# Sampling a 64 x 64 x 512 tensor along its sequence: matmuls with one-hot matrices, or gathers from DRAM

## What is computed

```python
x = x + L0(x, cond)   # modulated RMS norm, 16-head attention (q, k normed), projection
x = x + L1(x, cond)   # linear sampling, below
x = x + L2(cond, x)   # GRU over 64 steps
x = x + L3(cond, cond, x)   # Runge-Kutta steps of a coupled oscillator over 64 steps

# L1: input is x as (N, C, L) = (sequence, token, channel), grid is cond
ix = (grid + 1.0) * 0.5 * (L - 1)
x0 = jnp.floor(ix); w1 = ix - x0; w0 = 1.0 - w1
i0c, i1c = jnp.clip(x0, 0, L - 1), jnp.clip(x0 + 1, 0, L - 1)
v0 = jnp.take_along_axis(input, i0c[:, None, :], axis=2)
v1 = jnp.take_along_axis(input, i1c[:, None, :], axis=2)
return w0[:, None, :] * v0 + w1[:, None, :] * v1
```

## Time and profile before

| | us |
|---|---|
| median of 3 runs | 1828.99 |
| lowest, highest | 1824.32, 1829.84 |
| the profiled execution | 1831.36 |
| its span in the profile | 1829.4 |

### The profile page before, as it was taken

One profiled execution on the slowest core, in us unless ns is written; L12 is line 12 of the kernel. 1 busy time (PEld: TensorE's weight loads), 2 busy tenths in 40 slices (PEclk: granted clock), 3 DMA queues, 4 the chain that ended last, 5 costly groups with the idle time before them and its releaser, 6 DMA issues.

```text
span 1829.4 us, 100329 instructions
## 1 busy us (share of the span) xinstructions
PE 1593.6 (87%) x44506; PEld 1398.0 (76%) x44506; DVE 1582.0 (86%) x3935; ACT 821.4 (45%) x1886; POOL 697.0 (38%) x832
## 2 busy tenths in 40 slices
PE   5778778788878787885799999999999999999995
PEld 4355555556555555555799999999999999999995
DVE  5699999999999999986289888888988988899887
ACT  3533333323333333333255555555555555555553
POOL 2333333333333333334433444434443344434342
PEclk9889999999999999997799999999999999999999
DMA  5200010000000000002000000000000000000000
GB/s 183 93 16 23 25 25 18 24 23 25 26 25 17 25 23 26 20 13 80 6 10 14 13 14 16 14 13 14 13 15 15 13 13 15 15 14 13 14 15 15
DMA packets 91905, 45.47 MB, mean 25 GB/s; under 512 B 75984, under 2 KB 84240, under 8 KB 91472
## 3 DMA queue, kind: packets, MB, share of 16 engines
q1 hardware_dynamic: 91024, 39.03, 8.9%
q0 software_dynamic: 448, 0.02, 0.1%
HBM read 30.56 MB, written 8.45 MB: 21 GB/s over the span
## 4 chain that ended last, share of the span: by engine, by line
PE 49%; DVE 1%; issue 1%; POOL 0%; ACT 0%; POOLq 0%; ACTq 0%; DVEq 0%
PE ps_RZ L1032 20%; PE ps_F L1059 13%; PE ps_N L1032 10%; PE ps_F L1064 6%; DVE ps_S L1199 0%; DVE rest L1199 0%; DVE ts L1224 0%; DVE cub L1228 0%; ACT ps_T L1096 0%; POOL en L1337 0%; DVE ps_E L1199 0%; DVE qst L1199 0%; DVE Qs L1323 0%; DVE Hf L1220 0%; DVE P L1316 0%
## 5 line engine op out<-in xcount | busy, mean ns | idle before, releaser
L1059 PE MATMUL ps_F<-ts,Cp 128*128 128x64 f16 x8192 | 283.2, 193 | 12.7 <-ACT ts L1096 11.5
L825 PE MATMUL psQ<-Wx,front 128*128 128x512 f16 x1152 | 285.6, 401 | 1.2 <-issue 1.2
L1059 PEld LDWEIGHTS ps_F<-ts,Cp 128*128 128x128 f16 x8192 | 257.5, 98 | 14.6 <-ACT ts L1096 12.4
L634 DVE TENSOR_SCALAR E<-rows,lidx 128x512 f16<-128x512 f16 x512 | 229.4, 500 | 0.0
L1096 ACT ACTIVATE ts<-qst 128x256 f16<-128x256 f32 x192 | 80.1, 417 | 311.1 <-DVE qst L1199 311.1
L825 PEld LDWEIGHTS psQ<-Wx,front 128*128 128x128 f16 x1152 | 115.7, 103 | 133.7 <-issue 29.6
L1032 PE MATMUL ps_RZ<-xs,Wx 128*128 128x64 f16 x6144 | 204.0, 194 | 3.8 <-POOL xs L1341 2.4
L1032 PE MATMUL ps_RZ<-hs,Whh 128*128 128x64 f16 x6144 | 201.6, 193 | 1.3 <-POOL hs L1337 0.4
L1032 PEld LDWEIGHTS ps_RZ<-xs,Wx 128*128 128x128 f16 x6144 | 191.0, 99 | 5.5 <-POOL xs L1341 2.9
L1032 PEld LDWEIGHTS ps_RZ<-hs,Whh 128*128 128x128 f16 x6144 | 188.5, 98 | 2.4 <-issue 1.6
L1064 PE MATMUL ps_F<-ts,Cp 128*128 128x64 f16 x4096 | 163.0, 193 | 1.0 <-issue 0.3
(11 more groups left out here) (167 smaller groups left out, 3515.3 us busy)
## 6 DMA issues: line engine op xcount, KB each, us to landing
front<-in_x SPq DMA_DIRECT2D x32, 256.0 KB, 3.6
rows<-rows_dram SPq DMA_DIRECT2D x64, 128.0 KB, 3.0
out<-ot SPq DMA_DIRECT2D x512, 16.0 KB, 1.8
XR<-in_L_cond_W_qkv SPq DMA_DIRECT2D x4, 768.0 KB, 16.3
E<-in_L_cond_W_hh SPq DMA_DIRECT2D x4, 768.0 KB, 4.4
front<-in_L_cond_W_ih SPq DMA_DIRECT2D x4, 768.0 KB, 5.8
XR<-in_L_cond_W_emb SPq DMA_DIRECT2D x1, 2048.0 KB, 11.0
E<-in_L_cond_coupling SPq DMA_DIRECT2D x1, 1024.0 KB, 5.5
```

The source lines that it names most:

```text
L634: e = v.tensor_scalar(E[b][:, t, c, :], rows[b][:, :], lidx[:, t, c:c + 1], None, ALU.is_equal)
L825: last = mm(psQ[:, n, :], xn[p.u][:, i, c, :], Wqkv[:, j, c, n * D:(n + 1) * D], start=(c == 0 and t == 0), stop=(c == KC - 1 and t == 2))
L1059: mm(psF[:, s % 2, m, :], Cp[:, i, c, m * PART:(m + 1) * PART], ts_[:, 0, c, :], start=(c == 0 and m == 0 and i == 0), stop=False, skip_gr ...
```

## The change

The sampling is done by gathers instead of matmuls.

- After `residual`, x1 of a pair goes to DRAM (`store_x1` on SP, four DMAs of 128 KB): a buffer of 513 rows of 128 floats per sequence, in which row r holds channel r-1 in its left half and channel r in its right half, so that one row holds both taps for all 64 tokens.
- GpSimd issues 8 indirect DMAs per pair (`gather`), each fetching 128 rows of 512 bytes. They stand first in its slot, for pair i-3. The indices (`idx`) are transposed in `setup` as integers; i0 is capped at 510 with the weight going to the second tap.
- VectorE mixes the taps for pair i-4 in 16 instructions, `first_tap` and `second_tap`, within the Newton steps. The second writes XR.
- `residual` writes a contiguous tile x1; `keep_xT` writes one of five contiguous tiles. `build_tap`, `sample`, `weigh_taps`, `add_taps`, `high_x1`, `low_x1`, `load_rows` and E are gone. There is one slot more.
- x is loaded for pair i+3 instead of i+2.
- `setup` fills the four DRAM buffers with zeroes and waits for that.
- In the recurrences, the seeds and the bias are held narrow and are read with a stride of zero along the batch.

```diff
+        def store_x1(p):
+            sp.wait_ge(x1_done, p.n + 1)
+            for tap in range(2):
+                for b in range(2):
+                    rows = x1_dram[p.u * 2 + b][1 - tap:1 - tap + D, tap * T:(tap + 1) * T]
+                    sp.dma_start(rows.rearrange("(c p) t -> p c t", p=PART), x1[p.u][:, :, b, :]).then_inc(x1_out[p.u], 16)
...
         def slot(pair, i):
-            if p := pair(2):
+            if p := pair(3):
                 load_x(p)
...
-            if p := pair(-2):
-                load_rows(p)
...
             if i == NP:
                 for c in range(KC):
                     load_wih(c)
+            if p := pair(-2):
+                store_x1(p)
...
+        def gather(p):
+            pool.wait_ge(x1_out[p.u], p.half * 64 + 64)
+            pool.wait_ge(whh_lo, KC)
+            need(pool, x2_done, p.n - 1)
+            for b in range(2):
+                for c in range(KC):
+                    pool.indirect_dma_start(G[p.u][:, b, c, :], None, x1_dram[p.u * 2 + b],
+                                            bass.IndirectOffsetOnAxis(ap=idx[:, c, p.n * 2 + b:p.n * 2 + b + 1], axis=0))\
+                        .then_inc(gathered[p.u], 16)
...
         def slot(pair, i):
+            if p := pair(-3):
+                gather(p)
             if p := pair(1):
                 low_x(p)
...
-            if p := pair(-3):
-                add_taps(p, 0)
             if p := pair(-1):
                 norm_p(p)
-            if p := pair(-3):
-                add_taps(p, 1)
-            if p := pair(-2):
-                low_x1(p)
             if p := pair(2):
                 shift_x(p)
...
+        def first_tap(p, k):
+            b, c = k // KC, k % KC
             if k == 0:
+                dve.wait_ge(gathered[p.u], p.half * 128 + 128)
+                need(dve, x2_done, p.n)
+            v.scalar_tensor_tensor(out=um[:, b, c, :], in0=G[p.u][:, b, c, 0:T], scalar=WT[:, 0, c, p.n * 2 + b:p.n * 2 + b + 1],
+                                   in1=x1[p.u][:, c, b, :], op0=ALU.mult, op1=ALU.add).then_inc(tap0_done, 1)
+
+        def second_tap(p, k):
+            b, c = k // KC, k % KC
+            dve.wait_ge(tap0_done, p.n * 2 * KC + k + 1)
+            last = v.scalar_tensor_tensor(out=XR[:, :, c, p.n * 2 + b], in0=G[p.u][:, b, c, T:2 * T],
+                                          scalar=WT[:, 1, c, p.n * 2 + b:p.n * 2 + b + 1], in1=um[:, b, c, :],
+                                          op0=ALU.mult, op1=ALU.add)
             if k == 2 * KC - 1:
+                last.then_inc(x2_done, 1)
...
             for k in range(STEPS):
-                if tap and k + EARLY < 2 * KC:
-                    build_tap(tap, 1, k + EARLY)
+                if tap and k < 2 * KC:
+                    first_tap(tap, k)
+                if tap and k >= LAG:
+                    second_tap(tap, k - LAG)
```

More of the change, by code:

```diff
@@ L11 @@
 I32 = mybir.dt.int32
+U32 = mybir.dt.uint32
 WS = 64.0
@@ L60, in program @@
 def program(nc, x, cond, W_emb, b_emb, g_norm, W_qkv, g_q, g_k, W_out, W_ih, W_hh, b_ih, b_hh,
-            coupling, bias, out, rows_dram):
+            coupling, bias, out, x1_dram):
     B, T, D = x.shape
@@ L252, in _ @@
         last.then_inc(w1_T, 1)
+        pe.wait_ge(rows_ready, 1)
+        for c in range(KC):
+            last = nc.tensor.transpose(psI[:, c, :], irow[:, c * PART:(c + 1) * PART], ident[0:B, 0:B])
+        last.then_inc(idx_T, 1)
         pe.wait_ge(cond_kept, 1)
@@ L259, in _, with attention_and_sampling @@
         last.then_inc(emb_done, 1)
-def attention_and_sampling(nc, ctx, XR, ident, keep, later, x, rows_dram, W_out, coupling, W_hh, W_ih):
+def attention_and_sampling(nc, ctx, XR, ident, keep, later, x, x1_dram, W_out, coupling, W_hh, W_ih):
     B, T, D = x.shape
@@ L438, in norm_p @@
                 .then_inc(p_done, 1)
[L440 to L445, removed]
-            last.then_inc(x1_ready, 1)
         def shift_x(p):
@@ L592, in slot @@
                 keep_xT(p)
-            if p := pair(-2):
-                high_x1(p)
             if i == -1:
@@ L733, in slot @@
         def slot(pair, i):
-            x, qk, tap = pair(2), pair(0), pair(-3)
+            x, qk, tap = pair(2), pair(0), pair(-4)
             n = x.n if x else qk.n + 2 if qk else None
             cols = slice(QK.start if qk else X.start, X.stop if x else QK.stop)
-            for k in range(EARLY):
-                if tap:
-                    build_tap(tap, 1, k)
             if qk:
@@ L765, in slot @@
                 subtract_max(p)
-            if tap:
-                weigh_taps(tap, 0)
             if p := pair(-1):
                 sum_p(p)
-            if tap:
-                weigh_taps(tap, 1)
-            if p := pair(-2):
-                for k in range(2 * KC):
-                    build_tap(p, 0, k)
             if x:
@@ L922, in slot @@
                 project(p, 1)
-            if i == NP:
-                sample(pair(-3), 0)
-                sample(pair(-3), 1)
             if p := pair(-1):
@@ L933, in slot @@
                 scores(p)
-            if (p := pair(-3)) and i != NP:
-                sample(p, 0)
-                sample(p, 1)
             if p := pair(-2):
@@ L1445 @@
     out = nc.dram_tensor("out", shape, F32, kind="ExternalOutput").ap()
-    rows = nc.dram_tensor("rows_dram", (shape[0], shape[2]), F16, kind="Internal").ap()
+    rows = [nc.dram_tensor(f"x1_dram{k}", (shape[2] + 1, 2 * shape[1]), F32, kind="Internal").ap() for k in range(4)]
     program(nc, *args, out, rows)
```

145 lines of the change are left out of this document (50 added, 95 removed).

## The result

The changed kernel took **1949.97 us** (median of 4 runs, 1946.59 to 1953.59) against 1827.42 (4 runs, 1824.32 to 1829.84) for the kernel before: ratio 1.067, 95% interval 1.064 to 1.070. It is slower; the forecast was 1762, range 1700 to 1825. The kernel before takes much the same time in every job, 1821.6 to 1832.6; the changed one has two times, 1945.7 to 1950.0 in two jobs and 1720.8 in a third, and its executions in one job agree within 0.4%.

The account below looks back on a forecast made before the run. VectorE was taken to set the attention stage's 25.0 us slot. A period of 22.8 over 29 slots saved 64 us and the tail 3: 1831.4 - 67 = 1764, with the median 2.4 lower, 1762 us; range 1700 to 1825.

Parts of the forecast that it names:

- GpSimd's side: GpSimd's queue per slot: eight gathers at 1.1 us each, then `low_x`; costs nothing up to 1.6 us each.
- rival C: Gathers hold VectorE's Newton steps: 7 to 8 us more per slot, period near 29, about 1940 us; chance 0.08.
- Price of an issue: One indirect DMA issue on GpSimd: 1.1 us, bounds 0.5 and 3; eight take 8.8.
- Store: x1's way to DRAM, from `residual`'s end to the gathers' start: 6 us, bounds 3.0 and 12.
- Steps and taps: VectorE's Newton steps with 16 taps laced in: 6.45 us per slot, 2.3 of it for taps (bounds 1.6 and 4.5).
- Path and clock: Chain of waits through one slot: 21.55 us, plus 1.2 for TensorE's lower clock: period 22.8, bounds 21.0 and 25.
- Removal from VectorE: VectorE's work per slot: 7.35 us removed (sampling 6.7, `residual` 0.64), 2.3 added by the taps.
- Tail: End of the attention stage, after the last pair's `low_v`: 68.3 us becomes 65, so -3, bounds -12 and +15.
- the sum: Whole kernel: 29 slots save 64 us and the tail 3, so 1831.4 - 67 = 1764; median 1762 us.

Follow-up runs that it names:

- c1: The changed kernel itself, unchanged, timed again in another job on chip 12: 1720.8 us, ratio 0.943 to the kernel before.
- e7: The changed kernel with its 16 taps at the start of VectorE's slot, not among the Newton steps: 1946.5 us.
- e3: The changed kernel with the third `project` of a pair put between the two halves of `mix`: 1731.5 us.
- e11: The changed kernel with each of `mix`'s 96 matmuls using the whole array instead of a 64 by 32 tile (other values): 1959.8 us.

## Why the prediction was wrong

The gap to the kernel before is 1945.6 - 1829.4 = 116.2 us of span: 31 periods give (968.1 - 77.1) - 775.3 = 115.7, the rest 0.5. Against c1 it is 226.5: 31 periods give 891.0 - 672.6 = 218.4, or 7.0 a slot. The idle time ahead of L848 grew by more, 284.9 - 7.1 = 277.8 or 9.0 a slot: some 2 us a slot of it stand where TensorE is idle elsewhere in c1. That the "remote" part alone, 216.2, is near 218.4 is chance.

- **The step that failed** is "GpSimd's side". It gave the eight indirect DMAs a price in GpSimd's queue (1.1 each, "costs nothing up to 1.6") and on VectorE (rival C), and none on TensorE. They made the slot 7.0 us longer through TensorE on some chips, and held it not at all on others. The trace of before has no indirect DMA, so the price could not be read; but only two of the engines were bounded, and the others were taken as free.
- **Rival C** gave 1940 us and a period near 29, and 1950 and 28.7 were measured, with its mechanism false: the steps with all their taps took 518.81 to 524.41, 5.6 us, beside the gathers. The right number was luck.
- **Price of an issue**: pitch 1.25 (0.96 and 0.30 between), 10 us for eight instead of 8.8. It stayed free, as said: on c1 GpSimd waits 145.8 us in 31 slots for `rden`, 4.7 each.
- **Store**: from `residual`'s end to the first gather 4.2 us (519.85 to 524.04 in c1), 6 forecast.
- **Steps and taps**: 5.6 us measured, 6.45 forecast. In the kernel before, the 5.14 held 0.5 for the builds and 1.0 for the step under `low_x`, in every middle slot; in c1 and in the changed kernel no step is held in the middle slots, where I gave back only half (0.5). So the bare steps are 5.14 - 0.5 - 1.0 = 3.64, and sixteen taps cost some 2.0, 0.12 each; e7, with its taps elsewhere, has 3.6 from the first step to `scale_qk` in the median slot, against 5.4 with them, which gives 1.8. I took 2.3, within my bounds. The estimate by the formula of the Trainium skill's "VectorE: DVE Perf Modes", section on the TRN2 errata, was 3.6; the rows speak against it where independent instructions follow.
- **Path and clock**: c1's period is 21.70. The path summed to 21.55, and the 1.2 for TensorE's clock was added on top. The clock did fall as forecast (0.88, I said 0.90), so its cost is in the 21.70 and others were too large, the steps with their taps by 0.85 among them. That the rest agrees to some tenths is not shown term by term.
- **Removal from VectorE**: busy 91.39% of 25.0 = 22.8 us a slot before, 74.01% of 21.70 = 16.1 on c1: 6.8 less, where 7.35 - 2.3 = 5.05 was forecast; the hold of 1.0 that is gone is part of the rest.
- **Tail**: from the last `sum_p` to the end 1829.4 - 855.5 = 973.9 before, 967.4 on c1: -6.5, where -3 was forecast; 977.5 in the changed kernel.
- On c1 the whole is 1719.1 - 1829.4 = -110 us where the sum said -67: its 1720.8 us lie within the stated range, below the forecast's 1730 to 1800. The path held as far as the period shows it, and the largest mis-sized term is that period (21.7, not 22.8: 34 us over 31 slots).

## What to carry to other kernels

An instruction form that the trace of before doesn't hold has an unknown price on every engine, not only on the one that issues it; bound each, or run a small kernel with it first. Measure such a change on more than one chip, and put the two kernels that are to be compared into one job: a difference between jobs can be the chip's (e3's time looked like an effect of its order for two jobs). And when an instruction's cost is worked out from a stretch, take out of it first what else was held there: the 1.0 us of `low_x` would halve the price of the taps. Put long issues of GpSimd where its tensor instructions would otherwise meet VectorE's short two-input ones: by that the kernel with gathers was 0.9 us a slot faster than the one without, where TensorE wasn't held.

## What was not expected of the hardware

- Indirect DMAs of GpSimd (128 rows of 512 B, 0.96 us each) hold TensorE on some chips: after some 45 to 60 matmuls from the first issue, by the kernel, it goes on at one to four per 0.7 to 1.45 us, or not at all where it waits for its own semaphore, until the gathers are about through, with full-size tiles (e11) as with small ones. The same kernel took 1950.0 and 1945.7 us in two jobs and 1720.8 in a third.
- Direct DMAs of GpSimd with the same bytes (0.535 us each) don't, on either kind of chip: 1774.2, 1770.3 and 1775.4.
- Of the gathers' landing records in a trace, three quarters are missing where TensorE is held for eight gathers a slot (1,019 of 4,096 are there) and 6% in c1; with direct loads none.
- A tap of 0.32 us under a GpSimd tensor instruction of 1.27 took 1.23.
